# The residual of U4 added by transfer in phase 5 instead of phase 6, and phase 6's sums loaded later

## The reference

```python
h = conv1d(x, weight, kernel 9, padding 4, groups 4) + (cond @ c_weight.T)[:, :, None] + bias[None, :, None]
base = h @ kernel + ffn_bias                          # kernel is 2048 x 2048: the large product
A_eff, B_eff = gate-weighted sums of lora_A, lora_B   # rank 32, for groups of 4 samples
delta = (h @ A_eff.T) @ B_eff.T + (h @ lora_A_shared.T) @ lora_B_shared.T
out = x + base + delta                                # x is the residual
```

## Time and profile before

| | |
|---|---|
| time, median of 3 runs | 1656.8 us (1656.36 to 1657.97) |
| the profiled execution: its own time / its span | 1654.82 us / 1653.0 us |
| PE busy / DVE busy / ACT busy / POOL busy | 1641.2 / 1220.0 / 737.5 / 156.0 us |
| moved by DMA | 434.97 MB, mean 263 GB/s |
| PE busy in 1308 to 1473.3 us (14 steps of phase 5) | 165.30 of 165.30 us |
| DMA share in the same stretch | 0.92 |

### The profile page before, as it was taken

The page is one execution under the profiler, slowest core; times in us unless marked ns, Lnnn a source line. Parts: engine busy times, 40 slices in busy tenths (PEclk is TensorE's granted clock), DMA queues, the critical chain, the costliest instruction groups (busy, mean ns, idle before and its releaser), DMA issues. The chain is left out here.

```text
span 1653.0 us, 22362 instructions
## 1 busy us (share of the span) xinstructions
PE 1641.2 (99%) x8240; PEld 1401.2 (85%) x8240; DVE 1220.0 (74%) x1777; ACT 737.5 (45%) x978; POOL 156.0 (9%) x200
## 2 busy tenths in 40 slices
PE   9999999999999999999999999999999999999999
PEld 6799888898888899999998888887888888888887
DVE  7888888984465689999996545459989645567776
ACT  7766776744222575566661312144444311223221
POOL 0001001110152000000000134000000000001000
PEclk9999999999999999999999999999999999999999
DMA  8968777986887758877776798679999898998886
GB/s 249 282 225 289 259 247 257 318 279 183 288 308 269 239 187 295 288 253 242 255 261 216 254 322 309 235 226 250 268 268 244 293 328 316 315 317 259 230 230 172
DMA packets 192772, 434.97 MB, mean 263 GB/s; under 512 B 51956, under 2 KB 91476, under 8 KB 188024
## 3 DMA queue, kind: packets, MB, share of 16 engines
q1 hardware_dynamic: 170664, 353.69, 63.9%
q0 software_dynamic: 20992, 75.51, 17.1%
q10 hardware_dynamic: 1008, 4.34, 0.9%
HBM read 279.05 MB, written 154.42 MB: 262 GB/s over the span
## 5 line engine op out<-in xcount | busy, mean ns | idle before, releaser
L2295 PE MATMUL acc<-w_hi,y_t 128*128 128x512 f32 x2560 | 710.5, 391 | 2.4 <-DVE w_lo L1505 1.1
L2295 PEld LDWEIGHTS acc<-w_hi,y_t 128*128 128x128 f32 x2560 | 474.3, 188 | 98.1 <-issue 2.1
L2295 PE MATMUL acc<-w_lo,y_t 128*128 128x512 f32 x1280 | 395.5, 390 | 0.0
L2295 PEld LDWEIGHTS acc<-w_lo,y_t 128*128 128x128 f32 x1280 | 240.4, 188 | 51.2
L1131 ACT COPY x_q<-x_raw 32x512 f32<-32x512 f32 x248 | 269.6, 1087 | 20.4 <-DVE x_lo L1606 13.4
L2160 PE MATMUL cps<-cw,x_hi 128*128 128x256 f32 (+2 forms) x1088 | 244.1, 313 | 0.4 <-DVE x_lo L1799 0.4
L2160 PE MATMUL cps<-cw,x_lo 128*128 128x384 f32 (+2 forms) x768 | 181.1, 283 | 0.0
L2160 PEld LDWEIGHTS cps<-cw,x_hi 128*128 128x128 f32 x1088 | 176.5, 189 | 3.6 <-DVE x_lo L1799 1.2
L1176 ACT CAST y_t<-g 128x1024 fp32r<-128x1024 f32 x63 | 66.4, 1054 | 194.6 <-PE acc L2295 154.3
L1599 DVE COPY x_q<-x_raw 32x512 f32<-32x512 f32 x248 | 147.8, 596 | 4.4
L2160 PEld LDWEIGHTS cps<-cw,x_lo 128*128 128x128 f32 x768 | 135.2, 188 | 0.0
(11 more groups left out here) (243 smaller groups left out, 2190.7 us busy)
## 6 DMA issues: line engine op xcount, KB each, us to landing
g<-U SPq DMA_DIRECT2D x80, 512.0 KB, 7.3
A<-g SPq DMA_DIRECT2D x64, 512.0 KB, 4.4
g<-A SPq DMA_DIRECT2D x64, 512.0 KB, 5.7
x_raw<-in_x SPq DMA_DIRECT2D x31, 1024.0 KB, 5.2
U<-g SPq DMA_DIRECT2D x48, 512.0 KB, 5.2
g<-in_L_ffn_kernel POOLq DMA_DIRECT2D x32, 512.0 KB, 6.2
T<-g POOLq DMA_DIRECT2D x32, 512.0 KB, 4.6
g<-in_x SPq DMA_DIRECT2D x32, 512.0 KB, 6.5
```

Of the source, the lines that this page charges most:

```text
L2295: ins = T.matmul(acc[:, b, m, :], y_buf[b][:, c, part, :], wt[:, w, m * 512:(m + 1) * 512], start=(c == 0 and part == 0 and wt is w_hi), s ...
```

## The change

In phase 6 the residual is no longer added by POOL onto U4 in `pass_out`. POOL instead adds the same halves of `x` onto `u2_buf` in phase 5, after U2 has been loaded there and before `evac_u4` reads it, so that U4 is stored with the residual in it. `evac_u4` waits for that transfer (`u2_res`) and no longer for the load (`u2_in`). DVE's first additions in phase 6 wait for the load of U4 itself (`stage_in`). The loads of U4 for the next pass wait for the additions `E1` (first pair) and `P5B` (second pair) of the pass at hand, and the second of them is issued behind the first store of the pass. Phase 4 stays as it is.

```diff
@@ load_pass_out
                 if F == 6:
                     sp.wait_ge(u4_out[p % 2], 16 * (p // 2 + 1))
+                    if q >= 1:
+                        sp.wait_ge(pass_added, NADD * (r - 1) + (ADD_E1, ADD_P5B)[j])
                 sp.dma_start(pass_out[q % 2][j], (U3_d if F == 4 else U4_d)[p]).then_inc(stage_in[j], 16)
@@ SP, the passes of phase 6
                 if more:
                     load_b(first_pair(r + 1))
-                    for j in range(2):
-                        load_pass_out(r + 1, j)
+                    load_pass_out(r + 1, 0)
                 store_pass(r, 0)
+                if more:
+                    load_pass_out(r + 1, 1)
                 store_pass(r, 1)
@@ POOL
-            for r in range(2 * QS):
+            for r in range(QS):
                 for j in range(2):
                     u = first_pair(r) + j
-                    sample, c0 = (2 * (u % NP) + 1, 0) if r < QS else (2 * (u % NP), HALF)
                     pool.wait_ge(stage_in[j], 16 * ((u - NP) // 2 + 1))
                     if r >= 1:
                         pool.wait_ge(pass_added, NADD * (r - 1) + (ADD_E1, ADD_P5B)[j])
-                    V.dma_start(pass_out[r % 2][j], x[sample][:, c0:c0 + HALF], accum_op=ALU.add).then_inc(pass_res[j], 16)
+                    V.dma_start(pass_out[r % 2][j], x[2 * (u % NP) + 1][:, 0:HALF], accum_op=ALU.add
+                                ).then_inc(pass_res[j], 16)
+            for p in range(NP):
+                pool.wait_ge(u2_in[p % 2], 16 * (p // 2 + 1))
+                V.dma_start(u2_buf[p % 2], x[2 * p][:, HALF:L], accum_op=ALU.add).then_inc(u2_res[p % 2], 16)
@@ pass_add
                 if before is None:
-                    dve.wait_ge(pass_res[j], 16 * (r + 1))
+                    if r < QS:
+                        dve.wait_ge(pass_res[j], 16 * (r + 1))
+                    else:
+                        dve.wait_ge(stage_in[j], 16 * ((first_pair(r) + j - NP) // 2 + 1))
@@ evac_u4
-                dve.wait_ge(u2_in[pu % 2], 16 * (i // 2 + 1))
+                dve.wait_ge(u2_res[pu % 2], 16 * (i // 2 + 1))
                 V.tensor_tensor(u2_buf[pu % 2], acc_flat[pu % 2], u2_buf[pu % 2], ALU.add).then_inc(evac_u, 1)
```

More of the change, by code:

```diff
@@ L355, in build @@
         pass_res = [sem("pass_res0"), sem("pass_res1")]
+        u2_res = [sem("u2_res0"), sem("u2_res1")]
         pass_copied = sem("pass_copied")
```

## The result

The changed kernel takes 1675.41 us (median of 4 runs, 1673.25 to 1677.3), the kernel before 1656.97 beside it: 1.0115 times as long, with an interval of 1.0103 to 1.0126, 18.4 us slower. The forecast was 1671, with a range of 1656 to 1683. The profiled execution took 1673.25 us (span 1671.2).

The account below looks back on a forecast made before the run. PE bounds the kernel, with DMA close behind in phase 5 (share 0.92). Fifteen steps at 1.2 us over, less 4 us of cover, lose 14 us: 1671 us on the median's scale, range 1656 to 1683.

Parts of the forecast that it names:

- The bound, and that phase 6 has nothing to give: PE is busy 1641.2 of 1653.0 us; removing phase 6's 16 accumulating transfers wins at most 1.3 us, taken as 0.
- The moved loads of U4: Phase 6: the load of the next U4 waits for addition E1 and goes out some 6 us later, at cost 0.
- The price of a transfer: One accumulating transfer of 512 KB takes 2.92 us of all 16 DMA engines, read from phase 6.
- The sum of a step: Phase 5: DMA time per step with the new transfer, against PE's 11.81 us; 1.2 us a step over was taken.
- The upper end: Phase 5 step if plain packets' busy time cannot shrink: 13.80 us, 2.0 over PE's need, 26 us in all.
- the lower: Phase 5 step with the same traffic at 408 GB/s: 11.84 us, 0.03 over PE's need, 0 us in all.
- The cover of 4 us: Lateness phase 5 absorbs before PE waits, counted once: b_raw, first to be late, has 3.8 us to spare.
- their 5.6 us: Phase 5: spare time behind evac_u4 before the product that needs its PSUM half would be late, 5.6 us.
- Hidden: Rival for phase 5: the transfers shrink and PE never waits, time 1657 us, within 0.2%; chance 0.21.
- The limit by bytes: Form of the hidden rival: 4.31 MB a phase 5 step at 408 GB/s takes 10.6 us, under 11.81.
- The ring: Rival: U2's one-buffer cycle of store, load, accumulate and evac_u4 in phase 5 exceeds two steps; 1663 us, chance 0.12.
- the 10.5 that I asked for: Accumulate time in us from which the one-buffer cycle of phase 5 was to decide.

Follow-up runs that it names:

- E1: Not a run, and no run is called e1 in the kept text: DVE's phase 6 addition (first pair) that the load of U4 for the next pass waits for.

## Why the prediction was right

**The bound, and that phase 6 has nothing to give.** Right, and shown by the kernel without the transfers (0.9991). In the changed kernel phase 6 has no gap from 1550 to 1620 us at a share of 0.57, as forecast.

**The moved loads of U4.** Their cost of 0 was right, but a row was misread: what DVE starts at 1582.77 is the addition of U2. The addition E1 stands by itself, 7 us before it:

```profile
1575.64 0.69 DVE L1589 TENSOR_TENSOR g<-x_q,g 128x512 f32<-128x512 f32 x1
```

So the two loads of 1577.53 already stood behind E1, and the first of them did not move by 6 us: it goes out 0.8 us behind E1's start now, just as E1 ends, and 1.9 before. It is the second that goes out later, 10.4 us behind E1, as it waits for `P5B` and the first store. The 20 us from one pass to the next hold for E1 too.

**The price of a transfer.** 2.92 us by the rows of phase 6, 2.84 in its new place. Right.

**The sum of a step.** The upper end was 10.88 + 2.92 = 13.80 and the lower 11.84; I took 13.0. By the rows after, it is 3.78 MB x 2.71 = 10.2 us of plain traffic and 2.84 of the new, 13.1. The busy time of the plain packets did shrink, by 6%, perhaps as part of it had been waiting: of the way from the upper end to the lower, a third. (That the 6% had been waiting is my reading; no run separates the two.) This was the open quantity, and the step where I chose, 1.2 a step over, stands against 1.3. The choice was made between ends of 0.03 and 2.0, which mean 0 and 26 us, so that it came this near is in good part luck. Nor is the 13.1 an independent check of the length of a step: at a share of 1.00 the engines' time in a step is the step.

**The cover of 4 us.** 15 x 1.3 - 4 = 15.5; the fifteen stores of U4 show 14 steps of 12.91 instead of 11.81 us, 15.4 in all. The first gap came at 1353, in the fifth step (before the lora matmuls of the fourth product), which fits a cover of some 4 us, and at the place that I had named, `b_two`, with `evac_u4` late too but covered. That the evacuations come next was shown when `b_raw` went first; their 5.6 us no run measured.

**What was missing.** Two things. The entry to phase 6 cost 2.4 us more than before, where I had priced nothing. DVE is late there behind ACT, which waits 2.33 us for a piece of phase 6's matrix:

```profile
1508.45 1.05 ACT L1097 CAST w_hi<-st 128x1024 fp32r<-128x1024 f32 x1 [2.33 <-DMA st<-V]
```

Without any transfer in phase 5 there is no gap at that place, and with a quarter of each 0.78 us, so it goes with the traffic. DVE is busy without a pause from the `w_lo` that this made late (1509.53) to the last of the three gaps. That it is phase 5's backlog, handed on to these loads, fits but was not tested by itself. And PE's granted clock fell after two of the gaps, below. Two stretches of 13 us at 0.87 make about 3.4 us of the 5.2 by which PE's busy time grew, and they lie inside the steps of 12.91 us. But this was no second cost on top: with traffic, wait and phase 6's own transfers the clock stayed at 1.00 from 1308 to 1480 us and fell in the last 4 us of the same 14 steps only, and these were longer by 17.1 us. In a full stage a slower PE takes up time that it would else have waited, an explanation that I argue from these two traces only. The entry makes 2.4 of the 4.4 us between the forecast 14 and the 18.4 us, the steps 1.4.

**The rivals.** "Hidden" failed at the dose: it holds for a quarter of the transfer. The limit by bytes, at 408 GB/s, failed as well: the stage was full at 330. The figure of about 358 GB/s that I cited from the Trainium skill ("DMA: Bandwidth & Descriptors", Specifications) was not reached either; no run here held it over the stage (the most was 346 GB/s, with the plain transfers), and the table of doses goes by engine time, since a plain transfer and a half accumulating one differ by two in bytes and cost the same. "The ring" of one buffer had its condition nearly met, by another way than I wrote: the accumulates took 9.4 us, under the 10.5 that I asked for, but with store and load of the full stage the cycle is 1.23 + 7.2 + 7.9 + 1 + 9.4 = 26.7 us against 2 x 12.91. Still it is not what costs in the changed kernel: twice the ring gave nothing back, and the traffic without the wait cost as much. It follows from the full stage, and only with `b_raw` first did it add to the loss.

## What to carry to other kernels

Before a transfer is moved to a stage whose compute has room, add up that stage's DMA engine time in the profile: share times length, plus the price of the new transfer from a stage that has it. An accumulating transfer is to be counted twice against SP's plain ones (here 2.84 us against 0.524 x 2.71 = 1.42). When a stage is full, the wait that the profile names may only be the load that was served last, as here; to find out whether it is the cause, repeat the traffic with nobody waiting for it.

## What the runs showed of the hardware

The granted clock of TensorE fell after a gap of 3.17 us in the changed kernel. Busy time by stretch behind the gap that ended at 1380.24:

```profile
1380.00:1382.00 2.00, 1.76 (x7) 1.40 (x8) 2.00 (x3) 0.83 (x1) 0.00 (x0) 0.87 0.91 267
1382.00:1384.00 2.00, 2.00 (x6) 1.61 (x5) 2.00 (x3) 0.00 (x0) 0.00 (x0) 0.50 0.82 282
1384.00:1386.00 2.00, 2.00 (x8) 1.56 (x8) 1.85 (x2) 0.00 (x0) 0.00 (x0) 0.78 0.96 231
1386.00:1388.00 2.00, 2.00 (x11) 1.65 (x10) 0.00 (x0) 0.00 (x0) 0.68 (x1) 1.00 0.99 389
```

0.50 is the lower of its two levels, 1.2 for 2.4 GHz; PE does 6 matmuls in two us, where 759 in 172 us, at a clock of 1.00, make 8.8. The 13 us from 1380 show 0.87, and so do the 13 us behind the gap of 2.30 us at 1432. But in the same kernel no fall followed the gap of 2.52 us at 1486, in the kernel with traffic, wait and phase 6's own transfers a gap of 3.28 us, which ended at 1382.12, was followed by a clock of 1.00, and so was one of 2.53 us with `b_raw` first. The longest gaps in phase 5 were all followed by a fall: 3.51 us in the former of these two, 4.09 in the latter, 3.57 and 3.96 with the traffic alone, 4.78 with four buffers. What decides in the range of 2.3 to 3.3 us stays open.

Prices of accumulating transfers fall less than their size: 2.84 us for 4 KB rows, 1.73 for 2 KB and 1.02 for 1 KB rows, all of 128 rows. And a plain transfer of 512 KB took 1.71 us of the engines on POOL's queue in a full stage, where SP's plain traffic of the same stretch took 83.5% of 172 us for 52.15 MB, 1.44 us for as much; why, no run here tells.
